# Aligning TensorE's instruction stream to a slot of a 256-instruction block ahead of the first burst of scores, every fourth unit

## The reference, cut to what matters

```
for i in range(DEPTH):                                   # 6
    x = attn_layer(shift_tokens(x), Wqkv[i], ...) + x    # 16 heads of 64, windows of 32 tokens
    x = ffn_layer(shift_tokens(x), ...) + x              # 341 hidden channels, gelu gate

def attn_layer(x, Wqkv, qs, ksc, Wo):
    q, k, v = split(x @ Wqkv)
    q, k = rotary(l2norm(q) * qs), rotary(l2norm(k) * ksc)
    sim = einsum('bhwie,bhwje->bhwij', bq, look(bk)) * 8 # a window of 32 queries sees 64 keys
    attn = softmax(where(mask, -max, sim))
    return (attn @ look(v)).reshape(b, n, INNER) @ Wo
```

## Time and profile before

| | |
|---|---|
| time, 3 runs | 1716.12 us median (1715.34 to 1720.18) |
| the profiled execution | 1715.85 us |
| its span, first to last instruction | 1714.0 us |
| TensorE's mean granted clock | 0.984 |
| TensorE: products / weight loads busy | 1628.3 us (95%) / 1336.7 us (78%) |
| VectorE / ScalarE / GpSimd busy | 1480.7 (86%) / 1326.8 (77%) / 1331.4 us (78%) |
| packets of the queue "instruction" | 218 |

### The profile page before, as it was taken

The page is one execution under the profiler, slowest core; times in us unless marked ns, Lnnn a source line. Parts: engine busy times, 40 slices in busy tenths (PEclk is TensorE's granted clock), DMA queues, the critical chain, the costliest instruction groups (busy, mean ns, idle before and its releaser), DMA issues.

```text
span 1714.0 us, 66992 instructions
## 1 busy us (share of the span) xinstructions
PE 1628.3 (95%) x27395; PEld 1336.7 (78%) x27395; DVE 1480.7 (86%) x2314; ACT 1326.8 (77%) x2789; POOL 1331.4 (78%) x1798
## 2 busy tenths in 40 slices
PE   7999959999899999999999999998999999999997
PEld 5777647888788788788878878886888887888776
DVE  6887758999799899899989989997998998999884
ACT  6888746878688788788878778886887877788774
POOL 7777567888688788878878878887887888888770
PEclk9999979999999999999999999999999999999998
DMA  3588416565765656766567656657565566656554
GB/s 123 192 289 318 177 40 147 122 157 123 210 150 131 151 121 151 212 142 144 136 148 195 162 127 137 152 134 204 135 154 132 136 161 197 148 124 151 130 128 109
DMA packets 101393, 265.55 MB, mean 155 GB/s; under 512 B 26720, under 2 KB 34912, under 8 KB 101088
## 3 DMA queue, kind: packets, MB, share of 16 engines
q1 hardware_dynamic: 101088, 261.26, 60.5%
HBM read 45.15 MB, written 27.26 MB: 42 GB/s over the span
## 4 chain that ended last, share of the span: by engine, by line
PE 74%; POOL 5%; issue 4%; ACT 2%; DVE 1%; POOLq 0%; ACTq 0%; DVEq 0%
PE ps L1876 11%; PE ps L1878 9%; PE ps L1877 9%; PE ps L1936 9%; PE ps L1893 9%; PE ps L1915 7%; PE ps L1925 4%; PE ps L2005 3%; PE ps L1993 2%; POOL rot L1331 2%; PE ps L1995 2%; PE ps L1994 2%; PE ps L1907 2%; POOL rot L1389 1%; PE ps L1967 1%
## 5 line engine op out<-in xcount | busy, mean ns | idle before, releaser
L1331 POOL TENSOR_TENSOR rot<-rot 128x512 f32<-128x512 f32 x380 | 491.0, 1308 | 70.0 <-DVE rot L1466 70.0
L1466 DVE TENSOR_TENSOR rot<-ps,rope_l 128x1024 f32<-128x1024 f32 x380 | 463.0, 1219 | 28.9 <-ACT sq L1630 17.4
L1389 POOL TENSOR_TENSOR rot<-rot,rnorm 128x1024 f32<-128x1024 f32 x190 | 361.7, 1904 | 17.7 <-POOL rnorm L1359 0.4
L1876 PE MATMUL ps<-w_t,xs_hi 128*128 128x512 f32 x764 | 346.6, 454 | 18.8 <-PEq L369 11.1
L1640 ACT ACTIVATE un<-ps 128x512 f32<-128x512 f32 x384 | 229.4, 597 | 138.0 <-PE ps L1878 129.1
L1878 PE MATMUL ps<-w_t,xs_lo 128*128 128x512 f32 x764 | 305.8, 400 | 1.2 <-issue 1.2
L1877 PE MATMUL ps<-w_t,xs_hi 128*128 128x512 f32 x764 | 303.9, 398 | 0.0
L1630 ACT ACTIVATE sq<-ps 128x512 f32<-128x512 f32 x380 | 227.8, 600 | 46.8 <-PE ps L1878 38.1
L1452 DVE TENSOR_REDUCE ssum<-sq 128x16 f32<-128x1024 f32 x190 | 230.0, 1211 | 12.6 <-ACT sq L1630 12.6
L1893 PE MATMUL ps<-ident_s,rot 128*128 128x128 f32 x1536 | 234.0, 275 | 5.6 <-ACT kT L1656 4.1
L1893 PEld LDWEIGHTS ps<-ident_s,rot 128*128 128x128 f32 x1536 | 187.6, 141 | 62.6 <-issue 16.6
(11 more groups left out here) (152 smaller groups left out, 3323.5 us busy)
## 6 DMA issues: line engine op xcount, KB each, us to landing
vk<-un SPq DMA_DIRECT2D x1440, 128.0 KB
w_t<-weights_dram SPq DMA_DIRECT2D x48, 512.0 KB, 6.3
weights_dram<-rot SPq DMA_DIRECT2D x12, 1024.0 KB, 5.1
weights_dram<-sq SPq DMA_DIRECT2D x24, 512.0 KB, 3.8
raw<-wqk_dram SPq DMA_DIRECT2D x24, 256.0 KB, 4.4
wvt_s<-wvt_dram SPq DMA_DIRECT2D x12, 256.0 KB, 5.3
wo_s<-wo_dram SPq DMA_DIRECT2D x12, 256.0 KB, 5.5
w_s<-w_dram SPq DMA_DIRECT2D x6, 341.0 KB, 4.2
```

Source lines behind the costliest of these rows:

```text
L1331: last = G.tensor_tensor(cos[:, :, s, :], cos[:, :, s, :], sin[:, :, 1 - s, :], ALU.add)
L1389: G.tensor_tensor(v, v, rnorm[:, t, kind * H:(kind + 1) * H, None].broadcast_to([P, H, D]), ALU.mult).then_inc(nrm_g.sem, 1)
L1466: V.tensor_tensor(dst, src[:, None, :, :].broadcast_to([P, 2, H // 2, D]), tab[:, :, None, :].broadcast_to([P, 2, H // 2, D]), ALU.mult).t ...
L1876: M.matmul(bank, x_hi, w_t[:, j, 0, :], start=True, stop=False)
```

## The change

```diff
@@ -61,6 +61,7 @@
 HALF = 512
+FETCH_BLOCK = 256
@@ -1893,6 +1894,11 @@
+                def align_block(u):
+
+                    if live(u) and index(u) % 4 == 0:
+                        pe.addr_align(FETCH_BLOCK, offset=41)
+
@@ -2055,6 +2061,7 @@
                     feed_w1(last, 0)
                     if index(last) == UNITS - 1:
                         finish_turn(6)
+                    align_block(u)
                     proj(u, 1, 6)
                     scores(u, 0)
                     proj(u, 1, 7)
```

## The result

The changed kernel takes 1742.68 us (median of 4 runs, 1737.86 to 1744.54), the kernel before in the same comparison 1715.73 us (4 runs, 1713.33 to 1720.18). The ratio is 1.015, 95% interval 1.012 to 1.0179: 27 us slower, where +10 was forecast. The profiled execution is the shortest of the four: 1737.86 us, with a span of 1736.0.

What follows compares the result with a forecast made beforehand. TensorE was taken to set the pace, stopping where a block of 256 instructions hasn't arrived. -47 + 24 + 15 + 12 + 3 + 3 = +10 us on 1715.85 gave 1726 us, range 1698 to 1754.

Steps and rivals of the forecast that it cites:

- block that starts in the no-ops: Its successor, wanted 215 instructions later in mid-burst, comes late in two of eleven cases: 3 us, bounds 0 to 16.
- The no-ops: Ahead of proj(u, 1, 6), units 4 to 44: 51 ns each, less 1.15 us of lead, eleven times 1.1: 12 us.
- The first 140: No-ops ahead of the first aligned place, in unit 0: 7 us at 51 ns, 3 taken for slack; bounds 0 and 13.
- The second bursts: A block start at the end of each fourth unit's second burst of scores stops TensorE 2.0 us, twelve times: 24 us.
- After a weights load: Units 7, 15, 23, 31, 39: blocks fetched while DMA is full come late, 3.0 us five times: 15 us.
- The old stops: TensorE's waits for late instruction blocks in the kernel before, 2.0 us each, go, all but those ahead of unit 1: -47 us.
- cheap no-ops: Rival: no-ops under 26 ns each delay nothing at the aligned places; 1708 to 1714, 1711 us; chance 21%.
- Dear ones: Rival: no-ops at the aligned places cost as much as two waits in a row, a tenth of a us; 1760 us; 13%.
- the forecast's case: No-ops at the aligned places cost 35 to 75 ns each; 1717 to 1742 us; chance 48%.
- The good position: Rival: a block start at the second burst's very end costs only 0.27 us; 1687 to 1700, 1692 us; chance 14%.

Runs made afterwards that it cites:

- slot41_jump: The changed kernel with a branch over the no-ops (max_nops=0), so none is executed, block positions unchanged: 1705.35 us.
- slot41_small_loads: The changed kernel with its 40 weights loads of 512 KB cut to 16 KB each, so weights are not renewed: 1731.0 us.
- slot 12: The changed kernel with its twelve alignments to offset 12 instead of 41, no-ops still executed, 111 instead of 140 in unit 0: 1716.78 us.
- slot 91: The changed kernel with its twelve alignments to offset 91 instead of 41, no-ops still executed, 190 ahead of unit 0: 1776.93 us.
- slot12_jump: The changed kernel aligned to offset 12 instead of 41, with a jump over the no-ops (max_nops=0): 1681.26 us.

## Why the prediction came out as it did

The direction, the range (1698 to 1754) and all places but one held: 221 packets, 624 no-ops, stops at the end of each fourth unit's second burst, a pause at the aligned place in units 4 to 44, stops behind the five weights loads, and none of the old ones. Only the stops of the block that starts in the no-ops didn't come. The mechanism was the right one and a size was off. In the profiled execution units 1 to 46 take 1403.72 us against 1388.78, +14.9; unit 1 starts at 275.93, not 267.93, +8.0; the end gives 0.9 back; together +22.0. The forecast had +7 and +3 for the two.

- **The no-ops, 11 x 1.1 = 12: the step that failed.** I took the 51 ns recorded for a stand-alone wait as the price. The sequencer passes one each 71 ns, and 0.23 us more where a block starts: 3.2 to 3.5 us for 42 or 46. Less a lead of about 0.9 us (1.15 taken) that is 2.45 each: the recorded pause of 2.24 and the 0.2 that the modelled end hides. 27 us, 15 more than forecast. 71 ns lies within the 35 to 75 ns that I had allowed; with the block start and the first 140 it takes the time to the end of the forecast's own range (1742.68 against 1717 to 1742). `slot41_jump` takes both groups of no-ops away and leaves the positions as they are: 37 us.
- **The first 140, 3 of 7.** They took 10.3 us and unit 1 starts 8.0 later: +5. Some 3 us of the no-ops passed before TensorE needed the next product: it starts 7.3 us later, at 248.17 for 240.84. The waits behind it, on which I had counted as well, came again as they were (0.82, 0.52 and 1.30 us, before 0.82, 0.54 and 1.29), since the engines waited for had moved along.
- **The second bursts, 12 x 2.0 = 24.** Eleven stops of 1.65 us on average; with the hidden 0.2 and what the clock gives away about 24, an estimate as is the 11 of the next term. In unit 47 filler products follow and nothing stops. Right in sum.
- **After a weights load, 5 x 3.0 = 15.** 8.5 us recorded; with the same additions about 11. `slot41_small_loads` gives 9 to 12 from the other side.
- **The block that starts in the no-ops, 3.** No stop there at all. Only with fewer executed instructions ahead (the jump) or slot 12 does one come, at product 96 or 110. Counting gives a reason, which no run separates from others. At slot 41 the block is entered some 40 no-ops ahead of the place, and its successor is wanted about 5 us later; at slot 12 it is 12 no-ops, and about 3.3 us. The prediction's own reading of the kernel before was that blocks which last over 3.5 us end without a stop.
- **The old stops, -47.** All gone.

So 15 + 5 - 4 - 3 = 13 us were missing: 10 + 13 = 23, less the 0.9 at the end, is the +22.0 of this execution. The median is 27 higher; the other three executions have a granted clock of 0.979 to 0.981, this one 0.986, and in them I can't tell the stops one by one.

Of the rivals, cheap no-ops fell by the pauses. Dear ones came nearer than I gave them room for: 71 ns lies in the forecast's case, the 39 us at a tenth of a us each do not. The good position exists, but it is slot 12, not 41: at 41 a block starts within two instructions of the end of the fourth unit's second burst (127 or 128 products done), and such a start costs 1.26 to 2.52 us, not the 0.27 that this rival took.

The rule of the Trainium skill ("Runtime: NRT & Kernel Launch", instruction fetch mechanics) that fetching is hidden by the rate of issue is contradicted once more: between slot 91 and slot 12 lie 60 us, of which only some 6 are no-ops. Its warning that a taken branch forces a fetch is for a target outside the window of two pages. The jumps here lead into their own block or the next, so no run tests it; in `slot41_jump` and `slot12_jump` no product waited at the branch itself.

## What to carry to other kernels

Where an engine runs hundreds of very short instructions in a row, count its program in blocks of 256 and see where the starts fall; a recurring wait for "issue" at a fixed distance in instructions is the sign. If you move the starts, do it with something that the sequencer doesn't have to execute one by one, or in portions no longer than its lead, and choose the slot by the bursts of the whole period, not the first one. And take the price of an instruction from the distance between the starts of two in a row, not from its recorded duration.

## What the runs showed of the hardware that I had not expected

- A no-op on TensorE's queue is recorded at 13 ns and stands 71 ns behind its predecessor. Score loads with their products pass at 6.7 ns per instruction in the earlier trace rows: the cheapest instruction by record is ten times dearer than a load or a product.
- A taken jump into the next block is recorded for 0.28 to 0.31 us at slot 41, less than five no-ops take, and for 0.31 to 1.17 us at slot 12; no product waits for it at either. One that stays in its block was followed by stops of 0.2 to 1.8 us at the next two block starts.
- Waits for instructions can hang on data: with the weights loads cut to a 32nd, five stops and 9 to 12 us disappear.
- The clock can fall behind a pause at no-ops: at slot 12 it goes to its lower level (0.50 of full) behind six of the eleven, some 14 us in all; at the same slot with jumps or with spread no-ops it stays full from 270 to 1600 us.
- Some 24 us, 1.4% of the time, hang on nothing but the position of the program in its blocks: 1681.26 us at slot 12 and 1705.35 at slot 41, with the same jumps.
